# A fused cross-attention and feed-forward kernel: another order of its opening, with the low parts of W_r and W_v made on GpSimd

## What is computed

```python
# first block
h = rmsnorm(layernorm(x), g_res) @ W_in.T + b_in
s = scan(rmsnorm(ctx, g_init)[..., :512])          # s[t] = a * s[t-1] + u[t], decay a of about 1e-3
x2 = x + h + s[patch index of each row]            # a gather of rows of s
# second block
y = layernorm(x2); y_prev = y shifted down by one row
xr = mu_r * y + (1 - mu_r) * y_prev ; xk = mu_k * y + (1 - mu_k) * y_prev
out = x2 + sigmoid(xr @ W_r.T) * (relu(xk @ W_k.T) ** 2 @ W_v.T)
```

## Time and profile before

| what | before |
|---|---|
| median of 3 runs | 764.06 us (762.63 to 765.29) |
| profiled execution | 762.6 us |
| its span | 760.7 us |
| busy: TensorE, VectorE, ScalarE, GpSimd | 744.0, 586.7, 405.9, 173.2 us |
| mean granted TensorE clock | 0.995 of full speed |

### The profile page before, as it was taken

One profiled execution on the slowest core, in us unless ns is written; L12 is line 12 of the kernel. 1 busy time (PEld: TensorE's weight loads), 2 busy tenths in 40 slices (PEclk: granted clock), 3 DMA queues, 4 the chain that ended last, 5 costly groups with the idle time before them and its releaser, 6 DMA issues.

```text
span 760.7 us, 11065 instructions
## 1 busy us (share of the span) xinstructions
PE 744.0 (98%) x3432; PEld 613.7 (81%) x3433; DVE 586.7 (77%) x1063; ACT 405.9 (53%) x666; POOL 173.2 (23%) x163
## 2 busy tenths in 40 slices
PE   7987999999999999999999999999999999999998
PEld 4765888888888888888888888888888888888887
DVE  7789897887869768796876879777596977867462
ACT  4266464754545556453754545465363655544860
POOL 6533041313131031312113131121312113130000
PEclk9998999999999999999999999999999999999999
DMA  8685272726445273643616355281634627350011
GB/s 301 147 256 155 83 201 90 203 102 152 138 113 179 69 179 110 157 138 92 205 54 153 137 137 166 81 216 59 153 124 109 194 67 172 116 127 12 1 56 56
DMA packets 51453, 100.02 MB, mean 131 GB/s; under 512 B 5134, under 2 KB 5390, under 8 KB 51388
## 3 DMA queue, kind: packets, MB, share of 16 engines
q1 hardware_dynamic: 41900, 82.46, 31.3%
q0 software_dynamic: 9216, 16.78, 13.7%
q10 hardware_dynamic: 288, 0.27, 0.1%
HBM read 64.26 MB, written 21.76 MB: 113 GB/s over the span
## 4 chain that ended last, share of the span: by engine, by line
PE 92%; DVE 4%; issue 1%; POOL 1%; DMA 1%; ACT 1%; DVEq 0%; POOLq 0%
PE bank L561 29%; PE bank L562 29%; PE bank L563 29%; PE bank L681 3%; PE bank L775 1%; DVE scratch L1117 1%; DMA ring<-s_rows,patch_of 1%; POOL ring L499 0%; DVE bn_a L1013 0%; DVE xt_lo L984 0%; POOL rs_a L453 0%; DVE gate L1358 0%; ACT xr_hi L797 0%; DVE wk_lo L984 0%; DVE wi_lo L984 0%
## 5 line engine op out<-in xcount | busy, mean ns | idle before, releaser
L499 POOL DMA_INDIRECT ring<-s_rows,patch_now x60 | 99.3, 1655 | 229.0 <-DMA s_rows<-scanned 198.3
L1117 DVE SCALAR_TENSOR_TENSOR scratch<-turned,cols,scratch 128x512 f32<-128x512 f32 x128 | 94.5, 749 | 32.5 <-ACT scratch L846 13.6
L984 DVE TENSOR_TENSOR xr_lo<-scratch,xr_hi 128x512 fp32r<-128x512 f32 x124 | 85.1, 689 | 38.6 <-ACT xr_hi L797 37.9
L561 PE MATMUL bank<-xk_hi,wk_hi 128*128 128x512 f32 x256 | 101.2, 395 | 4.4 <-DVE xk_lo L984 4.3
L561 PE MATMUL bank<-wi_hi,xt_hi 128*128 128x512 f32 x256 | 101.5, 396 | 1.2 <-DVE xt_lo L984 1.1
L797 ACT ACTIVATE turned<-bank 128x512 f32<-128x512 f32 x64 | 33.1, 604 | 128.2 <-PE bank L681 128.2
L562 PE MATMUL bank<-xk_lo,wk_hi 128*128 128x512 f32 x256 | 100.8, 394 | 0.0
L563 PE MATMUL bank<-xk_hi,wk_lo 128*128 128x512 f32 x256 | 100.6, 393 | 0.0
L561 PE MATMUL bank<-wr_hi,xr_hi 128*128 128x512 f32 x256 | 99.8, 390 | 0.3 <-DVE xr_lo L984 0.2
L562 PE MATMUL bank<-wi_lo,xt_hi 128*128 128x512 f32 x256 | 99.7, 390 | 0.0
L563 PE MATMUL bank<-wi_hi,xt_lo 128*128 128x512 f32 x256 | 99.7, 389 | 0.0
(11 more groups left out here) (145 smaller groups left out, 1255.5 us busy)
## 6 DMA issues: line engine op xcount, KB each, us to landing
...
```

Source lines behind the costliest of these rows:

```text
L499: pool.indirect_dma_start(ring[b.slot][:, t, :], None, s_rows[:, :], bass.IndirectOffsetOnAxis(ap=rows, axis=0), compute_op=ALU.add).then_ ...
L561: nc.tensor.matmul(where, lhs_hi, rhs_hi, start=start, stop=False)
L984: return nc.vector.tensor_tensor(to, whole, high, ALU.subtract)
L1117: nc.vector.scalar_tensor_tensor(scratch[:, 2 + i % 2, :], turned[:, c, 1:S + 1], cols[:, 1 + which, c:c + 1], scratch[:, i % 2, :], ALU.m ...
```

## The change

1. VectorE no longer makes the low parts of W_r and W_v. GpSimd makes those of W_r in `root_b(0)`, behind the last root of batch 0 and ahead of the gathers of batch 1, and those of W_v at the head of its `iteration(0)`, behind these gathers. Each is one `tensor_tensor` subtraction of 128x512 float32 with both inputs and the output in SBUF. ScalarE makes the high parts of W_r later (after the squares of the context of batch 1) and those of W_v in two halves.
2. W_v is staged in `normed` instead of `gate`; the sigmoids don't wait for its low parts any more. Its load waits until batch 0 is transposed.
3. The context of batch 1 goes to the upper half of `scratch` instead of `ctx_rows` and is loaded, with x of batch 1, in the first microseconds; W_k is loaded without them.
4. VectorE takes the statistics of x of batch 1 earlier, makes the second half of `x_lo` of batch 1 ahead of `add_x` of batch 0, and reads the table of `far(0)` later. The mixes 2 and 3 of batch 0 stand ahead of the low parts of 2 and 3, and `far(1)` stands behind them.
5. The first key product goes in pairs of tiles, c outermost in each pair, and waits for the low parts of W_k one by one; VectorE makes them one by one between the mixes. The sigmoids stand between the mixes 5 and 6.
6. `root_c(1)` stands ahead of `root_b(0)`; `root_a(1)` stands ahead of all four gathers of batch 1, which no longer wait for single statistics.

```diff
-        staged = [gate, xt, ring[2], gate]
+        staged = [gate, xt, ring[2], normed]
...
+        def ctx_of(b):
+            return scratch[:, 2:4, :].rearrange("p a b -> p (a b)") if is_first(b, 1) else ctx_rows
...
             load_part(xt_of(Batch(0, 1)), x_turned[1], 0, C, xt_next_loaded)
+            load_x(Batch(0, 1))
+            sp.wait_ge(marks_counted, 1)
+            reached(sp, ms_c_done, Batch(0, 0), 1, 1)
+            load_ctx(Batch(0, 1))
+
             reached(sp, s_stored, Batch(0, 0), 16, 16)
             reached(sp, xt_lo_ready, Batch(0, 0), 2, 2)
             load_w(WR, w_r)
 
-            reached(sp, far_over, Batch(0, 0), 1, 1)
             rows_added(sp, Batch(0, 0))
-            load_ctx(Batch(0, 1))
-            load_x(Batch(0, 1))
-
             reached(sp, xt_lo_ready, Batch(0, 1), 2, 2)
             load_w(WK, w_k)
-            sp.wait_ge(w_lo_ready[WIN], C)
+            reached(sp, yn_turned, Batch(0, 0), T, T)
             load_w(WV, w_v)
...
@@ GpSimd: root_b(0), then iteration
+                    for c in range(C):
+                        pool.wait_ge(w_hi_ready[WR], c + 1)
+                        nc.gpsimd.tensor_tensor(wt_lo[WR][:, c, :], staged[WR][:, c, :], f32(wt_hi[WR][:, c, :]),
+                                                ALU.subtract).then_inc(w_lo_ready[WR], 1)
...
             def iteration(b):
                 nxt, new = b.plus(1), b.plus(2)
+                if is_first(b):
+                    for c in range(C):
+                        pool.wait_ge(w_hi_ready[WV], c + 1)
+                        nc.gpsimd.tensor_tensor(wt_lo[WV][:, c, :], staged[WV][:, c, :], f32(wt_hi[WV][:, c, :]),
+                                                ALU.subtract).then_inc(w_lo_ready[WV], 1)
                 if new.exists(B) and not is_first(nxt):
                     root_c(new)
                 if nxt.exists(B):
                     root_b(nxt)
-                if is_first(nxt):
-                    root_c(new)
-                if new.exists(B) and not is_first(nxt):
+                if new.exists(B):
                     root_a(new)
...
+            def first_key_product(b):
+                for pair in ((0, 1), (2, 3)):
+                    for c in range(C):
+                        pe.wait_ge(w_lo_ready[WK], c + 1)
+                        reached(pe, mix_lo_ready, b, 2 * C, C + c + 1)
+                        for m in pair:
+                            if c == 0:
+                                reached(pe, x2_ready, b.plus(1), T, m + 1)
+                            last = product(bank[m][:, :], wt_hi[WK][:, c, tile(m)], wt_lo[WK][:, c, tile(m)],
+                                           xk_hi[:, c, :], xk_lo[:, c, :], c == 0, c == C - 1)
+                            if c == C - 1:
+                                last.then_inc(k_done, 1)
...
@@ ScalarE: gates, iteration(0), iteration(-1)
-                    if is_first(b):
-
-                        act.wait_ge(w_lo_ready[WV], C)
...
                         mix_hi(b, C, C + 2)
+                        gates(b)
+                        mix_hi(b, C + 2, C + 3)
+                        weight_hi(WV, 0, 2)
+                        mix_hi(b, C + 3, 2 * C)
                         squares_c(new)
-                        mix_hi(b, C + 2, 2 * C)
-                        weight_hi(WV)
-                        gates(b)
+                        weight_hi(WV, 2, C)
...
                     x_hi(new, 1)
+
+                    reached(act, far_over, nxt, 1, 1)
                     squares_c(new)
+                    weight_hi(WR)
                     turned_out(nxt)
...
@@ VectorE: iteration(-1), then iteration(0)
-                    for t in range(T):
-                        add_x(nxt, t)
-                        statistics_b(nxt, t)
-                        if t == 1:
-                            x_lo(new, 1)
-                        if t == 2:
-                            early_stats_b(nxt)
+                    x_lo(new, 1)
+                    add_x(nxt, 0)
+                    statistics_b(nxt, 0)
+                    add_x(nxt, 1)
+                    statistics_b(nxt, 1)
+                    statistics_a(new, 2)
+                    stats_c(new)
+                    add_x(nxt, 2)
+                    statistics_b(nxt, 2)
+                    early_stats_b(nxt)
+                    statistics_a(new, 3)
+                    add_x(nxt, 3)
+                    statistics_b(nxt, 3)
                     late_stats_b(nxt)
                     norm_b(nxt, 0, T - 1)
-                    stats_c(new)
                     norm_b(nxt, T - 1, T)
                     scan_input(new)
-                    weight_lo(WR, 0, 2)
+                    stats_a(new, T)
                     mix_next(nxt, 0)
                     u_low(new)
                     mix_low(nxt, 0)
...
-                    weight_lo(WK)
-                    add_x(nxt, 0)
-                    mixing(b, C + 1, C + 3)
-                    stats_c(new)
-                    mixing(b, C + 3, 2 * C)
-                    add_x(nxt, 1)
-                    scan_input(new)
-                    weight_lo(WV)
+                    mix_next(b, C)
+                    weight_lo(WK, 0, 1)
+                    mix_low(b, C)
+                    add_x(nxt, 0)
+                    mix_next(b, C + 1)
+                    weight_lo(WK, 1, 2)
+                    mix_low(b, C + 1)
+                    add_x(nxt, 1)
...
                     add_x(nxt, 2)
                     add_x(nxt, 3)
+                    stats_c(new)
+                    scan_input(new)
                     clear_head(new)
                     stats_b(nxt)
                     ka_low(b, 0)
...
@@ VectorE: ahead of batches
             stats_a(Batch(0, 0), 3)
+            x_lo(Batch(0, 1), 0)
+            nc.vector.tensor_scalar(cols[:, 3:5, :], cols[:, 1:3, :], -1.0, 1.0, ALU.mult, ALU.add).then_inc(mus_ready, 1)
+            statistics_a(Batch(0, 1), 0)
+            statistics_a(Batch(0, 1), 1)
             far(Batch(0, 0))
             dve.sem_inc(far_over, 1)
-            x_lo(Batch(0, 1), 0)
-            nc.vector.tensor_scalar(cols[:, 3:5, :], cols[:, 1:3, :], -1.0, 1.0, ALU.mult, ALU.add).then_inc(mus_ready, 1)
             batches(dve, iteration, B)
```

42 lines of the change are left out of this document (19 added, 23 removed).

## The result

The kernel after the change takes 766.11 us (median of 19 runs, 765.33 to 767.55), the kernel before 763.1 us (19 runs, 761.64 to 766.68). The ratio is 1.0036, with a 95% interval of 1.0028 to 1.0044: slower, by 2.8 us, just above the 2.3 us that a measurement of this kernel can tell from no change. The profiled execution took 765.33 us with a span of 763.8 us, where before they were 762.6 and 760.7 us.

The account below looks back on a forecast made before the run. TensorE, busy 744 of 760.7 us, bounds the kernel, and VectorE its opening. The new order's -3.0 us and +3.3 us for engines holding each other make +0.3 us, so 764.4 us; range 762 to 767, whole range 760.0 to 768.5.

Parts of the forecast that it names:

- the mark: Start of the projection of batch 2, at 90.01 us before; what moves it was said to move the end as much.
- the third case: Rival, chance 0.14: GpSimd's subtraction is long, 2.1 us each, giving 772.4 us; its sign is batch 2's projection behind 93.
- the forecast: Chance 0.47: GpSimd and VectorE hold each other, +0.3 us in all, 764.4 us; its sign is batch 2's projection at 90.3.
- the one that I gave 0.04: Rival, chance 0.04: the early loads or another wait undo the gain in the opening, 765 to 767 us.
- part 1: VectorE's opening and the early loads: scan at 43.7 instead of 45.65, gate product 2.7 us earlier, loads taken as 0.
- Part 5: The subtraction on GpSimd, estimated from a select in the trace: 1.06 us for 512 elements.
- the rival of 2.1 us: Chance 0.14: each GpSimd subtraction takes 2.1 us because each input costs as much; with holding +8.3 us, 772.4 us.
- Part 6: GpSimd's subtractions and VectorE's operations hold each other, 0.91 us per held VectorE operation, +3.3 us together.
- the walk: Hand count of four engines' queues through the new order with trace spacings; the old order gave 90.4 for batch 2's projection.
- the engines run side by side: Rival, chance 0.27: GpSimd and VectorE do not hold each other, so -3.0 us, 761.1 us, from 760 to 762.
- Parts 2 and 3: Batch 1's gathers start at 49.8; the key product runs 56.5 to 70.5, 6.9 us won, some 3.5 from the clock.
- Part 4: Late next: squared keys' low parts, behind batch 2's root; VectorE idles 2.4 us, value product waits 1.3, 3.4 given back.

Follow-up runs that it names:

- f4: The changed kernel without its early loads: context and x of batch 1 behind the gathers of batch 0, VectorE's order as before up to the gate product; ratio 1.0053.
- e4: The changed kernel with GpSimd's low parts of W_r moved ahead of root_c(1), behind the gathers of batch 0; ratio to the kernel before 1.0045.
- e2: The changed kernel with the low parts of W_r back on VectorE, none of them on GpSimd; ratio to the kernel before 1.0046.
- e6: The kernel of e5 with the low parts of W_r back on VectorE; ratio to the kernel before 1.0045.
- e7: The kernel of e6 with the low parts of W_v on VectorE too, so none left on GpSimd; ratio to the kernel before 1.0053.
- e8: The kernel of e5 with GpSimd's low parts of W_r ahead of the roots of batch 0, root_c(1) between these roots; ratio to the kernel before 1.0041.
- e1: The changed kernel with x of batch 1 loaded behind the store of the first scan, its context still early; ratio to the kernel before 1.0039.
- e3: The changed kernel with the low parts of W_v back on VectorE, behind u of batch 2; ratio to the kernel before 1.0020.
- e5: The changed kernel with context of batch 1, W_r and x of batch 1 loaded behind the first scan's store, two statistics moved between additions; ratio 1.0062.
- f1: The kernel before with only the low parts of W_r moved to GpSimd, behind the roots of batch 0; ratio to the kernel before 1.0017.

## Why the prediction was right, and where it was not

**The result** lies in the range: 766.1 us where I said 764.4. The sign is less clear. By the line drawn in the prediction, 766.3 us, it is "the same", by 0.2 us; by the ratio it is slower, 2.8 us where the sum was +0.3. The two differ because the 764.06 us that the line was drawn from, a median of three runs, lies 1.0 us above the median of nineteen. At the mark it is +2.3 us where I said +0.3, and 92.3 is nearer to the prediction's sign for the third case (93) than to that for the forecast (90.3). The forecast's mechanism is there: both engines hold each other, and what the new order wins is given back. But so is the one that I gave 0.04, that the early loads undo part 1, at 765 to 767 us: that is where the first leg went. And the sum is as near as it is because errors of both signs meet in it, as the parts show.

**The step that failed is in part 1**, the early loads: "DMA is at a share of only 0.12 from 22 to 24 us, so I take 0; if the store is held until they are through, up to 1.0 us is lost". The share in these 2 us is what the queue leaves when nothing more is queued; it does not say what 1.5 MB more do to a store that goes out at 20 us. The store took 6.0 instead of 2.6 us, and the tiles were added 3 us late. 1.5 MB at the 402 GB/s of the stretch 20 to 22 us are 3.7 us. This sum could have been made from the trace of before, which reaches 409 GB/s in 46 to 48 us, and it was the bound to take, not 1.0 us. Whether a change without the early loads would be faster is not shown: f4, which has them late, is no faster, but its holds cost more.

**Part 5 was right in kind, small in size.** A subtraction of 128x512 takes 1.25 us (in e4, under `add_x` and statistics, they start 1.24, 1.26 and 1.25 us after each other; the last of a row shows up to 1.9), not 1.06. The estimate of 1.12 us by the Trainium skill (GPSIMD Engine Reference, Elementwise — side-by-side cycle accounting) was nearer than the select's rate, and still 10% short. Both inputs are thus read almost in the time of one; the rival of 2.1 us is out.

**Part 6 was right in kind.** Holds are seen where the walk had them: the normalizations, `u`, a mix and the last low part of W_k. Each costs 0.95 to 1.07 us (0.91 said), and they also take the small `TENSOR_SCALAR` of `v_a` (0.84 for 0.17), which the walk had as free. `add_x` and the statistics are free, as taken (e4). That the engines run side by side (0.27) is out.

**What of them arrives was wrong, and was offset by luck.** The walk goes from tile 3 to the scan in 6.8 us without holds and in 9.2 with them. The marks of the table give 9.1 to 9.2 us for it in the five variants of the change in which the low parts of W_r hold nothing on this way (e2, e4, e6, e7, e8), and 10.0 with the holds (after, e1, e3; 10.8 in e5, against 9.1 to 9.2 in e6 to e8). So the holds cost 0.8 us at the scan in the change and 1.6 in e5, not 2.4, and 2.3 us were missing from the walk for another reason. It says nothing of what e2 shows there: transposes at half the clock behind 4 to 6 us of idle time, with ScalarE's copies and the first mix behind them. That these make up all of the 2.3 us was not tried.

**Parts 2 and 3.** The scan's lateness, 49.87 against 46.1, is 3.8 us: 2.9 are there when tile 3 is added (39.83 against 36.9), by part 1, and 0.8 come between tile 3 and the scan. Everything behind it moved along, the first gather of batch 1 at 54.58 instead of 49.8 and the key product at 61.94 instead of 56.5. The clock went as forecast: 1.00 in 65 to 71 us where it was 0.55, though TensorE idled 2.38 us once. Not foreseen is the idle time ahead of the transposes, 4.57 us, and a clock of 0.54 behind it. That this, and not only the key product, is where the clock could fall was missing among the rivals.

**Part 4 was right in its waits.** The root behind the low parts of W_v is late next: VectorE idles 1.76 us ahead of `u` (2.4 said), and the value product waits for `ka_low` twice, 1.03 and 1.02 us (one wait of 1.3 said). From gate end to the mark the walk has 31.8 us without and 32.7 with holds; it is 30.6, so 2.1 us of the loss were made up here. This is not shown to be the new order's doing: f1, with the old order behind the gate product and only that product late, has 30.7.

**What the parts are worth**, as far as the ratios go: W_r on GpSimd +0.17% (f1, by itself); W_v on GpSimd +0.16% by e3 against after, but -0.08% by e6 against e7, so not even its sign is shown; W_v and the pairs together, with all that goes with them, +0.36% (f4 against f1). The early loads have no ratio of their own, since f4 moved the holds too. The parts are not additive: W_r back on VectorE gives nothing inside the change (e2), while the same edit gives 0.17% with the loads behind the store (e6 against e5). Each of these differences has an uncertainty of about 0.15 to 0.25%, so their order is not settled. What is settled is that none of the parts by itself, tried here, makes the kernel faster than before: all twelve ratios have intervals above 1.

**Left open**: how the loss divides between the early loads, W_v and the pairs, and whether part 1's reordering of VectorE would win by itself; none of these was tried alone.
